# One instruction stream per engine for all stages, the last query weights split in their own unit, down weights split in slices on two other engines, and matmul operands at chosen addresses

## The reference, cut to what matters

```
x = x + tanh(g0) * xattn0(layernorm(x), ctx)   # 32 heads, 8 kv heads, 64 context keys
x = x + tanh(g1) * ffn0(layernorm(x))          # silu(gate) * up, 1376 inner, then down
x = x + tanh(g2) * xattn1(layernorm(x), ctx)   # queries and keys rms-normed,
                                               # keys = 64 context + 256 own tokens
x = x + tanh(g3) * ffn1(layernorm(x))          # base matmul + top-2 of 28 rank-8 experts
```

## The kernel before, in words

| product, columns streamed | number of matmuls | moving, stationary |
|---|---|---|
| k/v weights w_kv x tokens xnT, 256 | 864 | 128, 128 |
| w_kv x context ctxT, both ways, 256 | 384 | 128, 128 |
| keys kT x queries qT (attention 1), 320 | 768 | 128, 128 |
| kvT x w0q, and WK x xnT (attention 0), 256 | 1152 | 64, 128 |
| w0o x kvT (attention 0), 512 | 192 | 128, 64 |
| VW x pT (attention 0), 512 | 384 | 64, 0 |
| all other products, 512 | 2984 | 128, 128 |

## Time and profile before

### The profile page before, as it was taken

One profiled execution on the slowest core, in us unless ns is written; L12 is line 12 of the kernel. 1 busy time (PEld: TensorE's weight loads), 2 busy tenths in 40 slices (PEclk: granted clock), 3 DMA queues, 4 the chain that ended last, 5 costly groups with the idle time before them and its releaser, 6 DMA issues.

```text
span 1426.1 us, 23791 instructions
## 1 busy us (share of the span) xinstructions
PE 1377.5 (97%) x7976; PEld 1195.4 (84%) x7976; DVE 1040.2 (73%) x2732; ACT 799.9 (56%) x2216; POOL 506.6 (36%) x626
## 2 busy tenths in 40 slices
PE   6999999999999998999999999999999999999998
PEld 5899998987778876888888888888888888888877
DVE  7777777787623337787788788787778778778775
ACT  6788777774211315565565565556556555656631
POOL 5865556654955612222222212122222221222220
PEclk8999999999999999999999999999999999999999
DMA  5221122211321300100101001001001001000001
GB/s 201 73 75 60 58 74 74 74 60 60 105 60 47 127 0 1 74 1 3 72 1 48 26 0 74 0 0 74 0 0 74 0 0 74 15 30 14 1 9 52
DMA packets 14942, 63.82 MB, mean 45 GB/s; under 512 B 1760, under 2 KB 1760, under 8 KB 10656
## 3 DMA queue, kind: packets, MB, share of 16 engines
q1 hardware_dynamic: 14880, 63.07, 12.5%
HBM read 60.97 MB, written 2.10 MB: 44 GB/s over the span
## 4 chain that ended last, share of the span: by engine, by line
PE 55%; DVE 5%; ACT 2%; issue 1%; POOL 0%; DVEq 0%; ACTq 0%
PE psum L57 16%; PE psum L59 15%; PE psum L58 15%; PE psum L1436 3%; PE psum L1447 2%; PE psum L1468 2%; PE psum L1431 1%; DVE w1q_lo L1054 1%; DVE v_lo L1133 1%; DVE pT_hi L1065 1%; PE psum L1544 1%; DVE pT_lo L1061 0%; ACT p L1302 0%; DVE dump L1125 0%; PE psum L120 0%
## 5 line engine op out<-in xcount | busy, mean ns | idle before, releaser
L1302 ACT ACTIVATE p<-psum,nb,rq 128x320 f32<-128x320 f32 x256 | 155.4, 614 | 149.4 <-DVE nb L1100 149.4
L1021 POOL TENSOR_TENSOR p<-p,rinv 128x640 f32<-128x640 f32 x64 | 80.2, 1253 | 203.6 <-DVE rinv L1106 203.6
L57 PE MATMUL psum<-w1q_hi,xnT_lo 128*128 128x512 f32 x288 | 120.2, 417 | 10.0 <-DVE v_lo L1133 7.3
L59 PE MATMUL psum<-w1q_hi,xnT_hi 128*128 128x512 f32 x288 | 114.0, 396 | 0.0
L58 PE MATMUL psum<-w1q_lo,xnT_hi 128*128 128x512 f32 x288 | 112.9, 392 | 0.0
L1096 DVE TENSOR_REDUCE mx<-psum 128x2 f32<-128x640 f32 x128 | 104.8, 819 | 3.4 <-PE psum L59 1.3
L1061 DVE TENSOR_TENSOR pT_lo<-psum,pT_hi 128x512 fp32r<-128x512 f32 x128 | 85.2, 687 | 28.4 <-ACT pT_hi L1279 26.9
L1279 ACT ACTIVATE pT_hi<-psum 128x512 fp32r<-128x512 f32 x128 | 69.6, 597 | 60.4 <-PE psum L1436 60.4
L57 PE MATMUL psum<-w1o_hi,oT_lo 128*128 128x512 f32 x256 | 100.4, 392 | 0.0
L58 PE MATMUL psum<-w1o_lo,oT_hi 128*128 128x512 f32 x256 | 100.3, 392 | 0.0
L59 PE MATMUL psum<-w1o_hi,oT_hi 128*128 128x512 f32 x256 | 99.7, 389 | 0.0
(11 more groups left out here) (235 smaller groups left out, 4645.0 us busy)
## 6 DMA issues: line engine op xcount, KB each, us to landing
raw_q<-in_w0q SPq DMA_DIRECT2D x8, 1024.0 KB, 4.8
raw_o<-in_w0o SPq DMA_DIRECT2D x8, 1024.0 KB, 4.8
raw_q<-in_w1q SPq DMA_DIRECT2D x8, 1024.0 KB, 7.5
raw_o<-in_w1o SPq DMA_DIRECT2D x8, 1024.0 KB, 4.9
raw_kv<-in_w_gu SPq DMA_DIRECT2D x10, 512.0 KB, 3.6
raw_gu<-in_w_gu SPq DMA_DIRECT2D x10, 512.0 KB, 3.6
raw_kv<-in_w0kv SPq DMA_DIRECT2D x8, 515.0 KB, 3.3
raw_kv<-in_w1kv SPq DMA_DIRECT2D x8, 512.0 KB, 5.5
```

The source lines that it names most:

```text
L57: pe.matmul(out, w[1], m[0], start=start, stop=False)
L59: return pe.matmul(out, w[0], m[0], start=False, stop=stop)
L1021: pool.tensor_tensor(p, p, k.rinv[:, stat(j)].unsqueeze(2).to_broadcast([PART, 2, KEYS]), ALU.mult).then_inc(p_scaled_pool, 1)
L1302: last = act.activation(k.p1[:, tile, 2 * hp + hh, :], s_pair(j)[:, hh, :], ACT.Exp, bias=k.nb[:, i:i + 1], scale=k.rq[:, i:i + 1], accum_ ...
```

## The change

Four edits, in the order of the code.

1. The three stages hand back their five engine functions and one Block calls them in turn. Where a stage's end protected a buffer or a PSUM bank, PE now waits for the thing itself (`ln.split`, `f0_x_done`). Two waits of attention 0's last group are set earlier, the gate and up banks of ffn 0 swap places, and SP's load for step 1 of ffn 0 stands in attention 0.
2. The down weights' hi is made by ACT and their lo by DVE, piece by piece (`DOWN`: two in steps 0 and 1, one in steps 2 to 8).
3. The first group's q split (`split_q`) stands in ffn 0, ahead of DVE's last x additions. The last two q pieces of the next group are split in unit 3, behind the two `x_add`.
4. Large buffers start on multiples of 256 bytes, and some start 192 bytes (`SHIFT` = 48 floats) or 128 bytes (`CTX_SHIFT`) past one: WK, kT of both attentions and w_kv by 192, ctxT by 128. Ffn 0 reads w_kv's buffer unshifted. The table of above becomes, in its order: 192, 0; 192, 128 and 128, 192; 192, 0; 192, 0; 0, 0; 0, 0; 0, 0.

```diff
+CTX_SHIFT, SHIFT = 32, 48
...
-                if not nxt and s == 6:
-                    pe.wait_ge(prep_free, base + OWN)
+                if not nxt and s in (6, 7):
+                    pe.wait_ge(prep_free, base + OWN + s - 8)
...
-    run(nc, sync, gpsimd, vector, scalar, tensor)
+    return sync, gpsimd, vector, scalar, tensor
...
+        sp.wait_ge(prep_full, HEAD + FILLS * (NKV - 2) + ORDER.index(("wk", 7)) + 1)
+        k.ffn0_gate_up(sp, 1)
...
-    gate_bank, up_bank, o_bank = [k.bank[0], k.bank[2]], [k.bank[1], k.bank[3]], k.bank[4:8]
+    gate_bank, up_bank, o_bank = [k.bank[2], k.bank[0]], [k.bank[3], k.bank[1]], k.bank[4:8]
+    DOWN = {0: [0, 1], 1: [2, 3], 2: [4], 3: [5], 4: [6], 5: [7], 6: [8], 7: [9], 8: [10]}
...
-            def dn(i):
-                j, p = i // 4, slice(0, width(i))
-                raw, i0, _ = DN[j]
-                pool.wait_ge(dn_hi, j + 1)
-                pool.tensor_tensor(k.w_dn[1][p, i, :], raw[p, (i - i0) * HID:(i - i0 + 1) * HID],
-                                   f(k.w_dn[0][p, i, :]), ALU.subtract).then_inc(dn_lo, 1)
...
+    def vector(dve):
+        def dn(i):
+            p, raw = slice(0, width(i)), down_raw(i)
+            dve.wait_ge(dn_hi, i + 1)
+            dve.tensor_tensor(k.w_dn[1][p, i, :], raw, f(k.w_dn[0][p, i, :]), ALU.subtract).then_inc(dn_lo, 1)
...
+            for m in DOWN.get(n, []):
+                dn(m)
...
+            if n == len(STEPS) - 1:
+                k.attn1_split_q(dve)
...
+        def dn(i):
+            p, j = slice(0, width(i)), i // 4
+            act.wait_ge(dn_in[j], 16 * len(dn_slices(*DN[j][1:])))
+            act.activation(k.w_dn[0][p, i, :], down_raw(i), ACT.Copy).then_inc(dn_hi, 1)
...
+            if n < 2:
+                pe.wait_ge(ln.split, NT + 4 + n)
...
+    def split_q(dve):
+        hi, lo = (w[:, :, :].rearrange("p a b -> p (a b)") for w in k.w_q)
+        dve.wait_ge(k.a1_in["q"], 16)
+        dve.tensor_copy(hi, raw["q"]).then_inc(k.a1_q_whi, 4)
+        dve.wait_ge(k.a1_q_whi, 4)
+        dve.tensor_tensor(lo, raw["q"], f(hi), ALU.subtract).then_inc(k.a1_q_wlo, 4)
...
-                    if b == 0 and not first:
-                        w_lo("q", g, 2)
-                        w_lo("q", g, 3)
...
                     if prev:
                         x_add(u, b, 0)
+                    for c in conv[4:5]:
+                        w_lo(*c)
                     scale_p(n, 2)
                     if prev:
                         x_add(u, b, 1)
+                    for c in conv[5:6]:
+                        w_lo(*c)
...
-                w_lo("q", NKV, 2)
-                w_lo("q", NKV, 3)
...
+            if not prev:
+                pe.wait_ge(k.f0_x_done, NT - 1)
...
+            if not prev:
+                pe.wait_ge(k.f0_x_done, NT)
...
+            if not prev:
+                pe.wait_ge(ln.split, 2 * NT + 6)
...
-        def pair(scope, name, shape):
-            return [sb(scope, name + part, shape, F32R) for part in ("_hi", "_lo")]
+        def pair(scope, name, shape, shift=0):
+            flat = [sb(scope, name + part, [shift + math.prod(shape)], F32R)[:, shift:] for part in ("_hi", "_lo")]
...
+        k.ctxT = pair(stack, "ctxT", [CH * BATCH * CTX], CTX_SHIFT)
...
+        w_kv = [sb(stack, "w_kv" + part, [SHIFT + KVW], F32R) for part in ("_hi", "_lo")]
+        k.w_kv, k.w_gu0 = [w[:, SHIFT:] for w in w_kv], [w[:, 0:KVW] for w in w_kv]
...
+            k.WK = pair(scope, "WK", [CH, BATCH, GH, CTX], SHIFT)
+            k.kvT = [pair(scope, "kT0", [BATCH * CTX], SHIFT), pair(scope, "vT0", [BATCH * CTX])]
...
-    k.kT = pair(scope, "kT1", [BATCH, CTX + SEQ + CTX])
+    k.kT = pair(scope, "kT1", [BATCH, CTX + SEQ + CTX], SHIFT)
```

More of the change, by code:

```diff
@@ L463, in prep @@
                 j = fill[1]
-                last = act.activation(k.kvT[0][:, j, :], bank[:, 0:BATCH * CTX], ACT.Identity,
+                last = act.activation(k.kvT[j][0][:, :], bank[:, 0:BATCH * CTX], ACT.Identity,
                                       bias=k.bias[:, GH + j:GH + j + 1])
@@ L571, in prep @@
                                [w[:, 2 * hp + h, c * PART:(c + 1) * PART] for w in wq4],
-                               [w[:, 0, :] for w in k.kvT], True, True)
+                               [w[:, :] for w in k.kvT[0]], True, True)
             else:
@@ L578, in prep @@
                     pe.wait_ge(o_lo, CONV["o"] * g + h + 1)
-                last = mm3(pe, bank, [w[:, 1, pr * PART:(pr + 1) * PART] for w in k.kvT],
+                last = mm3(pe, bank, [w[:, pr * PART:(pr + 1) * PART] for w in k.kvT[1]],
                            [w[:, h, :] for w in wo4], True, True)
@@ new lines, in kv_evac, with body @@
+                        last = act.activation(k.v[0][half, b + i, 2, :],
+                                              y_bank(b, "cx")[64 * i:64 * i + 64, HD:2 * HD], ACT.Copy)
+                last.then_inc(cx_hi, 1)
+        def body(g, first, nxt):
+            for b in range(BATCH):
+                n, prev = BATCH * g + b, not (first and b == 0)
+                u, conv = n - 1, pieces(g, b)
+                if prev:
+                    for tile in ln_tiles(u)[1:]:
+                        ln.act_hi(act, *tile, ln_bank(b - 1, 1))
+                    t_evac(u, b, 2)
+                if not (first and b == 1):
+                    kv_evac(g, b)
+                if prev:
+                    t_evac(u, b, 3)
+                    t_evac(u, b, 4)
+                    pv_evac(u, b, 0)
+                if b == 1 and not first:
+                    act.wait_ge(d_full, 2 * u)
+                if conv:
+                    w_hi(*conv[0])
+                q_copy(n, b, 0, not prev)
+                act.wait_ge(kt_full, n + 1)
+                bank = x_bank(b, "k")
+                last = act.activation(k.kT[0][:, b, CTX:KEYS], bank[:, 0:SEQ], ACT.Copy, scale=k.qkw[:, 0:1])
+                if b % 2 == 0:
+                    for at in (slice(0, CTX), slice(KEYS, KEYS + CTX)):
+                        last = act.activation(k.kT[0][:, b:b + 2, at], two(bank[:, SEQ:SEQ + 2 * CTX]),
+                                              ACT.Copy, scale=k.qkw[:, 0:1])
+                last.then_inc(kt_hi, 1)
+                if prev:
+                    t_evac(u, b, 5)
+                if conv:
+                    w_hi(*conv[1])
+                for late in ln_tiles(n):
+                    ln.act_norm(act, *late)
+                q_copy(n, b, 1, not prev)
+                q_hi(n, b, 0, not prev)
+                for c in conv[2:4]:
+                    w_hi(*c)
+                if prev:
+                    pv_evac(u, b, 1)
+                q_hi(n, b, 1, not prev)
+                exps(n, 0)
+                exps(n, 1)
+                for c in conv[4:]:
+                    w_hi(*c)
+                exps(n, 2)
+                if not prev:
+                    kv_evac(g, 1)
+                t_evac(n, b, 0)
+                t_evac(n, b, 1)
+                for tile in ln_tiles(n)[:1]:
+                    ln.act_hi(act, *tile, ln_bank(b, 0))
+                exps(n, 3)
@@ new lines, in build, with _ @@
+        with nc.Block() as block:
+            @block.sync
+            def _(sp):
+                a0[0](sp)
+                f0[0](sp)
+                a1[0](sp)
+            @block.gpsimd
+            def _(pool):
+                a0[1](pool)
+                f0[1](pool)
+                a1[1](pool)
+            @block.vector
+            def _(dve):
+                a0[2](dve)
+                f0[2](dve)
+                a1[2](dve)
+            @block.scalar
+            def _(act):
+                a0[3](act)
+                f0[3](act)
+                a1[3](act)
+            @block.tensor
+            def _(pe):
+                a0[4](pe)
+                f0[4](pe)
+                a1[4](pe)
```

1395 lines of the change are left out of this document (655 added, 740 removed).

## The result

The changed kernel took 1409.21 us (median; 1409.04 to 1412.08) against 1426.8 us for the kernel before beside it: ratio 0.9882, 95% interval 0.9869 to 0.9895. It is faster by 17.6 us. I had forecast 29, and the time lies 1.2 us above the range.

What follows compares the result with a forecast made beforehand. PE, busy 1377.5 of 1426.1 us, bounds the kernel. -7.2 - 3.8 - 3.5 - 3.7 - 10.2 = -28.4 us from 1427.87 gives 1399.5, a median of 1397.6, with small waits 1397; range 1389 to 1408.

Steps and rivals of the forecast that it cites:

- part 1: Last q pieces moved to unit 3: seven v_lo waits in attention 1 go, -7.2 us; ffn 1's start, -3.8 us.
- part 4: Operand addresses: matmul steps shorten at other residues modulo 256, -10.2 us in all, between 0 and -17.5.
- the second pushes pT_lo by at most its own 0.65: Attention 1, unit 3: the second moved w1q_lo subtraction delays pT_lo by no more than its 0.65 us.
- the cap of 4.5 us: Attention 1's groups: if DVE does not catch up in unit 3, at most 7 x 0.65 = 4.5 us is lost.
- Ffn 1's start: The 2.6 us w1q_lo wait and 1.7 us of half clock behind it go, 0.5 given back: -3.8 us.
- Part 2: Stage boundaries: attention 1 starts 1.8 us earlier, ffn 0 1.7 us earlier, nothing replaces these waits: -3.5 us.
- Part 3: Ffn 0's weights: PE's waits for late operands go, and DVE's added subtractions are covered by PE's step: -3.7 us.
- four waits: PE's waits in ffn 0: 0.9 us for w_gu_lo, 1.7 for f_h, 0.6 and 0.5 for POOL, all gone.
- 6.4 ns: Gain per 256-column matmul from residues 64 and 128 (0.1136 us) over 128 and 128 (0.120), carried to other products.
- Rival B: Whole kernel: addresses do nothing, since the distance that matters is not the one read; 1407.8 us, chance 0.18.
- rival C: Waits return one step on: pT_lo late in unit 3 (4.5 us), ffn 0 uncovered (3.3 us); 1405, chance 0.12.
- the chances of A to D: Forecast itself 0.55, addresses do nothing 0.18, waits return 0.12, all address bounds met 0.12; given together as 0.96 faster.

Runs made afterwards that it cites:

- the third experiment: The changed kernel with q pieces 2 and 3 back in the next group's unit 0 and at ffn 1's start: 1414.9 us, ratio 0.9915.
- Both pieces early: The changed kernel with both w1q_lo pieces of unit 3 together ahead of the reciprocal that lets POOL's scale start: 1404.11 us, ratio 0.9844.
- the second piece late: The changed kernel with unit 3's second w1q_lo piece moved behind the last row maximum and pT_lo on DVE: 1404.43 us, ratio 0.9840.

## Why the prediction was wrong

The sum said -28.4 us against the profiled execution; the spans gave -15.8. Two steps failed: the price of the pieces' new place (part 1) and the addresses (part 4). Part 3 gave more than I had counted.

**Part 1, groups: -7.2 forecast.** The waits for v_lo fell from 7.3 + 0.6 to 6.3 us: -1.6 (by PE's starts 8.5 gained, 6.8 lost). The step that failed is "the second pushes pT_lo by at most its own 0.65", and with it the cap of 4.5 us. I took 0.65 from a row in which POOL was idle, and it was 1.32 where it was put. I also gave the chain behind the maximum time until the next unit, and it had 0.14 us: I had followed it to the scale and the turned tiles, and not to ACT's copy of the batch's own v. The Trainium skill (SBUF, Who interferes with whom), which I had quoted for part 3 only, says that a DVE instruction with two SBUF inputs waits out a GpSimd one that reads SBUF and holds the port. The rows here agree: the piece ended 0.56 after POOL's scale, nearly all of the 0.68 that it takes alone. DVE's x addition beside the same scale, with one input from PSUM, took 0.73.

**Ffn 1's start: -3.8 forecast, -3.8 in the stretch.** That the two agree is in part luck. The 2.6 us of the wait are the edit's, worth 2.9 by starts. The clock gave some 1.5 between the two profiles, and the third experiment shows that the gap alone does not bring it. Against them stand the new waits at the turned tiles, 1.4 in rows and 1.5 by starts, for which I had given back 0.5; one group's change and the steps make up the rest.

**Part 2: -3.5 forecast.** Both boundary waits are gone and nothing took their place; PE's starts moved together by 1.9 and 2.0 us there: right, as far as the rows tell. It was not tried by itself.

**Part 3: -3.7 forecast, some -6.** Ffn 0 shrank by 8.0, 2.0 of it the second boundary. The mechanism was right and the size too small, for two reasons. I priced four waits by their rows, 3.7 us; by the starts of the same matmuls before and after they were worth 1.2, 0.85, 2.0 and 0.8, 4.8 in all. And I left out two short ones, 0.3 us each in rows and 0.5 by starts, for a turned tile and w_kv_lo. Taking the part back cost 5.1 us in the trace; the late load, which did not come back, was the 1.2, and the turned tile lost 0.5 more in that run than it had before. The eleven subtractions on DVE took 19.2 us, not 7.2, and each of them ended 0.54 or 0.55 us after an instruction of POOL that ran beside it. Groups of the changed kernel in ffn 0 (line, engine, names, shapes, count; busy us, mean ns; idle before), ten of the eleven:

```profile
L756 DVE TENSOR_TENSOR w_dn_lo<-raw_q,w_dn_hi 128x512 fp32r<-128x512 f32 x6 | 9.7, 1644 | 0.0
L756 DVE TENSOR_TENSOR w_dn_lo<-raw_o,w_dn_hi 128x512 fp32r<-128x512 f32 x4 | 8.4, 2090 | 0.0
```

Here the same collision costs PE nothing that a row shows: its only wait left in ffn 0's window is 0.3 us for k_raw. The subtraction stands last in DVE's step, behind the activation, and the step of PE, 5.4 us, covers it. That is the difference between parts 1 and 3.

**Part 4: -10.2 forecast, -1.5 to -1.9 in the trace.** Summed over the steps inside even runs that the traces hold, w_kv x xnT gave -2.3 to -2.5, the products of w_kv and ctxT -1.2 (as forecast), w0o some -0.4, WK x xnT and kvT x w0q together +1.8, and the others +0.6. On the chip, old against new map is 0.2 to 1.4 us at like clock, from single executions at each. The step that failed is the carrying over of 6.4 ns from one pair of rows. Over the whole trace before, that pair is 119.8 against 114.5 to 115.0, so even there it is 5 and not 6.4. w_kv gained 3.4 of it, kT x qT, for which I had no row at another distance, nothing, VW nothing; and WK, which I priced at nothing for its unchanged distance, lost 2.7 ns in each of 768. Rival B (1407.8) was nearest in number, for a part of the right reason; rival C supplied the rest.

**The sum again,** by the starts of the same matmuls in the two traces: the boundaries -3.9, ffn 0's waits -5.9, v_lo in the groups -1.7, ffn 1's start -2.9. In the changed kernel's profile the half clock at 544 us lasted 6.8 us where it had lasted 3.4 before (at 557), +1.0. That is -13.4 of the -15.8; the remaining 2.4 are the steps of part 4, 1.5 to 1.9, and small differences at the start of attention 0, where the half clock also lay differently.

One slip in the forecast: the chances of A to D add up to 0.97, not 0.96. Nothing else hangs on it.

**A version that beats both.** Both pieces early, with the changed kernel's addresses 1404.11 us, with those of before 1402.78 us: ratios 0.9844 and 0.9831. Between the two the intervals do not decide, nor against the second piece late (0.9840).

## What to carry to other kernels

Before an instruction is moved, list what the other engine runs at its new place: a duration read beside an idle neighbour doesn't hold beside a busy one. Then ask what stands next in its new queue, follow that chain to the engine that bounds the kernel, and read how late it may be; both pieces in DVE's idle time cost PE nothing, and the second of them 0.9 us later on its queue gave 7 of the 10 us back. And price a wait of PE by the starts of its matmuls, with and without it, since the row leaves out up to 0.3 us of each. A difference between two operands' steps is a row about those two until a third operand has shown it.

## What the runs showed of the hardware

- Steps of 256 fp32r columns depend on where the operands lie: 119.5 to 119.8 ns with equal residues modulo 256, 114.5 to 117.7 with unequal ones, means over even runs. The estimate of 109 ns from the Trainium skill (TensorE: Matmul & The Clock Gate, Wait, 56ns, not 53.3ns?) is reached by none of them. What sets the values between 114.5 and 117.7 stays open.
- A DVE subtraction of 512 columns with both inputs in SBUF took 0.68 us alone, 1.32 when it began 0.49 us into POOL's scale, and 1.64 to 2.09 on average in ffn 0 beside POOL's splits. The 19 stretched ones in the changed kernel's trace (8 in attention 1, 11 in ffn 0, 0.95 to 2.93 us each) ended 0.54 to 0.55 us after a POOL instruction that was running beside them. A DVE x addition with an input from PSUM, beside the same scale, took 0.73.
- A wait of PE costs more than its row: 1.97 us for 1.74, 1.21 for 1.03, 0.89 for 0.74, by the starts of matmuls.
- The mean granted clock of one kernel was 0.999 in some executions and 0.995 in others, at 2 to 3 us more. In traces the half clock in attention 1's first units lasted 6.8 us in the two profiles of the changed kernel and was absent with both pieces early. Behind a wait of 2.6 us it came in one profile and stayed away in another, of a kernel with other parts changed.
